# Comparisons for four users at a time in four slots, in place of eight users in two slots

## The chip, the cores and the metric

The kernel runs on one core of one Trainium2 chip. The metric is the device time of one execution in microseconds (us). A core has the matrix engine TensorE (PE in the rows; its weight loads are PEld), VectorE (DVE), ScalarE (ACT), GpSimd (POOL) and SyncE (SP). They run their own instruction streams and meet at semaphores. On-chip memory is SBUF (128 partitions) and PSUM, which TensorE writes. Tensors in DRAM are moved by DMAs, which here are issued by SP and by POOL.

## The reference

For 2048 users with a history of 200 item numbers each and 50 retrieved items each, over a table of 12500 items x 512:

```
mask = (sequence_ids != 0)
seq_emb = where(mask, item_embeddings[clip(sequence_ids - 1, 0)], 0)
pooled = seq_emb.sum(axis=1) / max(mask.sum(axis=1), 1)
user_rep = pooled @ W_rec.T + b_rec
retrieved = item_embeddings[retrieved_indices].mean(axis=1)
gate = sigmoid(concat([user_rep, retrieved]) @ gate_W.T + gate_b)
fused = gate * user_rep + (1 - gate) * retrieved
logits = fused @ proj_W.T + proj_b            # 2048 x 12500
```

## The kernel before

The histories are not gathered. Per user the kernel counts how often each of the 12544 table rows (98 chunks of 128) occurs, and multiplies the table by these counts. An item number is split into a chunk number and a row in the chunk. For each user, DVE compares the row keys of the 200 items with the numbers 0 to 127 and the chunk keys with 0 to 97 (`make_hots`, L568 and L570); TensorE multiplies the two zero-one matrices, which gives the 128 x 98 counts of that user (`count_quad`, L931, two matmuls a user), four users ("a quad") in one PSUM bank of three; ScalarE moves a quad to SBUF as bytes (`move_quad`, L779).

`make_hots(n)` makes one unit of 8 users: a DVE instruction of 2048 elements a partition into `row_hots` and one of 1568 into `chunk_hots`. There are two slots, so unit n waits until the quads of unit n-2 are counted (`quad_counted`). There are 4 groups of 512 users, each with 128 quads or 64 units.

The work runs in stages:

- Phase 0: group 0 is counted, with nothing to pool yet. The hots of all 64 units are made one after another. ScalarE squares a piece of the table after each seventh quad (L785), 14 times.
- Passes 0 to 3: pass g pools group g over 49 chunk pairs, 16 matmuls of 512 columns each pair (`pool_half`, L949), and in passes 0 to 2 TensorE counts the next group's quads between the half pairs (`quads_by`). On DVE, `units_by(i)` says how many units are made by iteration i of the pass. In pass 0 DVE also splits the table (`split_low`, L575). At the end of passes 0 and 1 DVE prepares the keys of the group after next (`prepare_ids`, L544 to L557), makes that group's first two units, and only then moves the pooled sums out of PSUM (`move_pooled`, L593), for which TensorE waits in the next pass.
- Logits: 400 blocks of 12 matmuls of 500 columns (L1022), moved by DVE (L755).

Beside this the 50 retrieved rows of each user are gathered by indirect DMAs from POOL, in program order. In a "lane" (`gather_lane`, L468 and L471) the DMA itself adds to what is there; there are 4 lanes of 50 gathers, two in phase 0 and pass 0, then one each during passes 1 and 2. The other blocks are gathered in batches of two (`gather_batch`, L449) into a pool of slots and added by DVE (`add_batch`, L610), 44 adds in pass 1 and 44 in pass 2, one after the hots of nearly each iteration. A batch that finds no free slot waits for an add. Turns of the first lanes wait for hots (L487), so that they are spread over phase 0 and pass 0. In pass 1 a turn of four lane gathers stands in front of each third batch until the lane is done.

Of the kernel before, what the change touches and what calls it, by code (L numbers as in the profile page):

```python
# [7 lines left out]
F16 = mybir.dt.float16  # L8
I32 = mybir.dt.int32
U8 = mybir.dt.uint8  # L10
ALU = mybir.AluOpType
# [3 lines left out]
P = 128  # L15
# [1 line left out]
KH = 4  # L17
H = 512
QUAD = 4
UNIT = 8  # L20
RING = 6
STAGE = 3
CVT = 3
# [28 lines left out]
class Plan:  # L52

    def __init__(self, seq_len, top_k, users, items, hidden):
# [7 lines left out]
        self.quads = G // QUAD  # L62
        self.units = G // UNIT
        self.width = next(n for n in range(512, 0, -1) if items % n == 0)
# [11 lines left out]
        return max(0, min(self.quads, (2 * i + half - 5) * self.quads // 90))  # L76

    def units_by(self, i):
        return min(self.units, self.quads_by(i + 1) // 2 + 1)

    def place_batches(self):

# [39 lines left out]
def pooling_program(nc, pl, ids, ret_ids, emb, w_rec_t, b_rec, w_gate_t, b_gate, proj_t, proj_b,  # L122
                    emb_parts, pool_dram, ret_dram, out):
    NQ, NP, NG, NB, K = pl.chunks, pl.pairs, pl.groups, pl.blocks, pl.top_k
# [4 lines left out]
    with ExitStack() as scope:  # L129
        def sem(name):  # L130
            return scope.enter_context(nc.semaphore(name))

        def sb(name, shape, dt):
            return scope.enter_context(nc.sbuf_tensor(name, shape, dt))
# [5 lines left out]
        keys = sb("keys", [P, 12288 + 2 * 8 * NQ * 2 * 2], U8)  # L140
        row_hots_t = sb("row_hots", [P, 2 * 8 * P * 2], F16)
# [20 lines left out]
        def part_of(tile, at, bytes_, dt):  # L162
            return tile[:, at:at + bytes_].bitcast(dt)
# [8 lines left out]
        clamped = part_of(keys, 4096, 4096, I32)  # L172
        row_key = part_of(keys, 8192, 2048, F16)
        chunk_key = part_of(keys, 10240, 2048, F16)
        chunk_hots = part_of(keys, 12288, 2 * 8 * NQ * 4, F16).rearrange("p (s k c v) -> p s k c v", s=2, k=8, v=2)
        row_hots = row_hots_t[:].rearrange("p (s k c v) -> p s k c v", s=2, k=8, v=2)
        present = sb("present", [P, 2 * G], F16)

        side = 2 * NQ * G // 2
# [52 lines left out]
        hots_made = sem("hots_made")  # L232
        quad_counted = sem("quad_counted")
# [67 lines left out]
        def adds_by_pass(g, i):  # L301

            if g <= 0:
                return 0
            return ADDS_PASS[g - 1] + min(ADDS_PASS[g] - ADDS_PASS[g - 1], (i + 1) * (ADDS_PASS[g] - ADDS_PASS[g - 1]) // 47)
# [123 lines left out]
        def _(pool):  # L429
# [31 lines left out]
            def gather_lane(block, turn):  # L461

                lane = block if block < LANES else 0
                for n in range(turn * LANE, min(turn * LANE + LANE, K)):
                    a = n % LANE
                    to, landed = gathered[:, lane * LANE + a], sum_in[lane][a]
                    if turn == 0:
                        pool.indirect_dma_start(to, None, source, column(block, n)).then_inc(landed, 16)  # L468
                    else:
                        pool.wait_ge(landed, lane_landed(block, a) - 16 * len(range(a, K, LANE)) + 16 * turn)  # L470
                        pool.indirect_dma_start(to, None, source, column(block, n), compute_op=ALU.add).then_inc(landed, 16)  # L471
# [12 lines left out]
            turns = -(-K // LANE)  # L484
            for turn in range(turns):
                if turn > 0:
                    pool.wait_ge(hots_made, 9 * turn)  # L487
                for block in range(LANES):
                    gather_lane(block, turn)
            pool.wait_ge(ret_rows_made, 2)  # L490
# [49 lines left out]
        def _(dve):  # L540
            def prepare_ids(g):
                dve.drain()
                dve.wait_ge(ids_in, 16 * (g + 1))
                dve.tensor_scalar(chunk_of, raw, -1.0, None, ALU.add)  # L544
                dve.tensor_scalar(chunk_key, raw, 0.0, ABSENT, ALU.is_equal, ALU.mult)
                if g > 0:
                    dve.wait_ge(present_counted, g)
                dve.tensor_scalar(present[:], raw, 0.0, None, ALU.not_equal)
                dve.drain()
                dve.tensor_scalar(clamped, chunk_of, 0.0, float(pl.items - 1), ALU.max, ALU.min)  # L550
                dve.drain()
                dve.tensor_scalar(raw, clamped, P - 1, None, ALU.bitwise_and)
                dve.tensor_scalar(clamped, clamped, 7, None, ALU.logical_shift_right)
                dve.drain()
                dve.tensor_tensor(row_key, raw, chunk_key, ALU.add)
                dve.drain()
                dve.tensor_copy(chunk_key, clamped)  # L557
                dve.drain().then_inc(ids_ready, 1)

            def make_hots(n):  # L560

                u = n % pl.units
                if n >= 2:
                    dve.wait_ge(quad_counted, 2 * (n - 1))
                rk = row_key[:, u * 16:u * 16 + 16].rearrange("p (k a v) -> p k a v", a=1, v=2)
                ck = chunk_key[:, u * 16:u * 16 + 16].rearrange("p (k a v) -> p k a v", a=1, v=2)
                cols = pair_columns[:].rearrange("p (a c) v -> p a c v", a=1)
                dve.tensor_tensor(row_hots[:, n % 2], cols.broadcast_to((P, 8, P, 2)),  # L568
                                  rk.broadcast_to((P, 8, P, 2)), ALU.is_equal)
                dve.tensor_tensor(chunk_hots[:, n % 2], cols[:, :, 0:NQ].broadcast_to((P, 8, NQ, 2)),  # L570
                                  ck.broadcast_to((P, 8, NQ, 2)), ALU.is_equal).then_inc(hots_made, 1)

            def split_low(i):
                dve.wait_ge(high_made, i + 1)
# [97 lines left out]
            dve.drain()  # L672
            dve.tensor_scalar(last_row, last_row_i, float(pl.items - 1), None, ALU.add)
            prepare_ids(0)
            make_hots(0)
            make_hots(1)
            def make_ret_rows(first, last):

                at = slice(first * K, last * K)
# [12 lines left out]

            dve.wait_ge(ret_ids_in, 16)
            make_ret_rows(0, LANES)
            for n in range(2, pl.units):
                make_hots(n)
                if n == 57:
                    dve.wait_ge(norm_summed, 1)
                    dve.tensor_reduce(small[:, 0:1], pooled_ps[:, 0, 0:NORM], AX.X, ALU.add)
                    dve.drain()  # L700
                    scale_from_squares(dve, small[:, 0:1], expo[:], small[:, 1:2], small[:, 2:3])
                    dve.drain().then_inc(scale_made, 1)
# [2 lines left out]
            split_low(2)  # L705
            prepare_ids(1)
            make_ret_rows(LANES, NB)
            make_hots(pl.units)
            make_hots(pl.units + 1)

            for g in range(NG):
                if g > 0:
                    move_pooled(g - 1)
                    make_recip(g)
                made = 2
                for i in range(NP):
                    if g == 0 and i == 0:
                        make_recip(0)
                    if g == 1 and i < LANES:
                        finish_lane(i)  # L720
                    if g >= 2 and i == 1:
                        finish_lane(g)
                    if g + 1 < NG:
                        while made < pl.units_by(i):
                            make_hots((g + 1) * pl.units + made)
                            made += 1
                    if g == 0 and i + 3 < NP:
                        split_low(i + 3)
                    before = adds_by_pass(g, i - 1) if i > 0 else adds_by_pass(g - 1, NP - 1)
                    for k in range(before, adds_by_pass(g, i)):  # L730
                        add_batch(k)
                    if g == NG - 1:
                        dense_step(i, MIX_PASS, SUM_PASS, LOW_PASS)
                        if i == 38:
                            scale_strip(0)
                        if i == 42:
                            low_strip(0)
                if g + 2 < NG:
                    prepare_ids(g + 2)
                    make_hots((g + 2) * pl.units)  # L740
                    make_hots((g + 2) * pl.units + 1)
            move_pooled(NG - 1)
            dve.drain()
            scale_out(0)
# [2 lines left out]
            for n in range(LAST):  # L747
                t, j = divmod(n, HALF_BLOCKS)
                r, v = divmod(n, ROWS)
# [161 lines left out]
        def _(pe):  # L911
# [8 lines left out]
                last.then_inc(present_counted, 1)  # L920

            def count_quad(q):
                pe.wait_ge(hots_made, q // 2 + 1)
                if q >= COUNT_BANKS:
                    pe.wait_ge(quad_moved, q - COUNT_BANKS + 1)
                slot = q // 2 % 2
                for u in range(QUAD):
                    pair, v = divmod(q % 2 * QUAD + u, 2)
                    to = count_ps[:, q % COUNT_BANKS, u * NQ:(u + 1) * NQ]
                    for part in range(2):  # L930
                        last = pe.matmul(to, row_hots[:, slot, pair * 2 + part, :, v],  # L931
                                         chunk_hots[:, slot, pair * 2 + part, :, v],
                                         start=(part == 0), stop=(part == 1))
                last.then_inc(quad_counted, 1)
# [184 lines left out]
```

## Time and profile before

| | |
|---|---|
| median of 3 runs | 2339.99 us (2335.43 to 2343.23) |
| profiled execution | 2341.4 us, its span 2339.7 us |
| mean granted TensorE clock | 0.949 |
| PE busy | 92% of the span |
| DVE busy | 64% |
| POOL busy | 48% |
| phase 0 (to the first pooling matmul) | 0 to 156 us |
| pass 0 | 156 to 388 us |
| pass 1 | 391 to 656 us |
| pass 2 | 661 to about 917 us |
| pass 3, then logits | to 1177 us, then to the end |

The stage borders are where the pooling matmuls of one pass end and those of the next begin in the timeline. A busy share is an average over stages with different limits, so each stage has to be read by itself.

### The profile page before, as it was taken

How to read it: one execution, taken by the hardware profiler on the slowest of the kernel's cores; microseconds unless marked ns; L12 is line 12 of the kernel's file. 1: busy time of each engine (PE TensorE's matmuls, PEld its weight loads, DVE VectorE, ACT ScalarE, POOL GpSimd, SP SyncE). 2: the span in 40 equal slices, each digit the busy share in tenths (PEclk: the TensorE clock that was granted, in tenths of full speed). 3: DMA queues.
4: the chain of work that ended last, by engine and by line, in shares of the span. 5: the costliest groups of instructions: out<-in, count | busy, mean ns of one | idle time of the engine just before them, and what ended most of it. 6: DMA issues, size and time to landing. Idle time of an engine off the chain costs nothing. (4 is left out here: it accounts for less than half of the span.)

```text
span 2339.7 us, 31173 instructions
## 1 busy us (share of the span) xinstructions
PE 2157.0 (92%) x12548; PEld 1099.0 (47%) x12548; DVE 1491.0 (64%) x1701; ACT 717.6 (31%) x947; POOL 1123.8 (48%) x830
## 2 busy tenths in 40 slices
PE   5669999888899888999999898999999999999999
PEld 4545555444545444444444343444444444444444
DVE  8998999676788766334477775876444444443343
ACT  6856775343444333222311111221121100111110
POOL 5673541888858888757368887788000000000000
PEclk7569999999999899999999999999999999999999
DMA  9998995999978999969588898888524445544553
GB/s 303 333 198 273 311 316 202 267 245 236 256 238 263 233 252 280 373 226 344 169 270 297 292 305 255 287 283 295 188 92 159 161 160 172 171 166 157 169 171 115
DMA packets 205198, 554.76 MB, mean 237 GB/s; under 512 B 20992, under 2 KB 104192, under 8 KB 201728
## 3 DMA queue, kind: packets, MB, share of 16 engines
q1 hardware_dynamic: 127424, 334.62, 41.3%
q0 software_dynamic: 77632, 218.16, 34.1%
q8 instruction: 101, 1.65, 0.3%
q14 instruction: 41, 0.34, 0.0%
HBM read 416.21 MB, written 136.48 MB: 236 GB/s over the span
## 5 line engine op out<-in xcount | busy, mean ns | idle before, releaser
L949 PE MATMUL pooled_ps<-mid,ring 128*128 128x512 f16 x3136 | 749.3, 388 | 20.9 <-DVE mid L593 7.9
L449 POOL DMA_INDIRECT gathered<-emb,ret_rows x462 | 565.9, 1225 | 236.8 <-issue 135.3
L755 DVE SCALAR_TENSOR_TENSOR ring<-pooled_ps,out_scale,counts 128x500 f32<-128x500 f32 x320 | 235.3, 736 | 355.4 <-PE pooled_ps L1022 351.0
L949 PEld LDWEIGHTS pooled_ps<-mid,ring 128*128 128x128 f16 x3136 | 298.3, 100 | 346.0 <-issue 54.4
L1022 PE MATMUL pooled_ps<-counts,keys 128*128 128x500 f16 x1920 | 427.5, 380 | 13.9 <-DVE ring L755 11.7
L471 POOL DMA_INDIRECT gathered<-emb,ret_rows x184 | 346.9, 1885 | 145.7 <-DVE keys L570 81.5
L1022 PE MATMUL pooled_ps<-counts,mid 128*128 128x500 f16 x1920 | 411.8, 374 | 0.0
L931 PE MATMUL count_ps<-keys,row_hots 128*128 128x98 f16 x4096 | 289.0, 228 | 108.1 <-DVE keys L570 92.6
L568 DVE TENSOR_TENSOR row_hots<-pair_columns,keys 128x2048 f16<-128x2048 f16 x256 | 312.6, 1221 | 60.3 <-PE count_ps L931 59.4
L931 PEld LDWEIGHTS count_ps<-keys,row_hots 128*128 128x128 f16 x4096 | 257.4, 109 | 191.9 <-DVE keys L570 108.7
L610 DVE TENSOR_TENSOR gathered<-gathered 128x1024 f32<-128x1024 f32 x182 | 223.2, 1226 | 158.0 <-DMA gathered<-emb,ret_rows 145.5
L779 ACT ACTIVATE counts<-count_ps 128x392 uint8<-128x392 f32 x512 | 237.6, 491 | 261.3 <-PE count_ps L931 261.2
L1022 PEld LDWEIGHTS pooled_ps<-counts,keys 128*128 128x128 f16 x1920 | 188.8, 100 | 240.9 <-issue 21.6
L861 ACT ACTIVATE counts<-counts,strip_scale 128x2000 f16<-128x2000 f32 x50 | 98.1, 1961 | 639.2 <-PE pooled_ps L1022 358.8
L1022 PEld LDWEIGHTS pooled_ps<-counts,mid 128*128 128x128 f16 x1920 | 186.8, 97 | 218.6
L803 ACT ACTIVATE mid<-counts 128x1024 f16<-128x1024 uint8 x196 | 205.9, 1054 | 184.9 <-PE pooled_ps L949 184.1
L570 DVE TENSOR_TENSOR keys<-pair_columns,keys 128x1568 f16<-128x1568 f16 x256 | 247.8, 968 | 0.0
L1022 PE MATMUL count_ps<-counts,keys 128*128 128x500 f16 x480 | 112.4, 385 | 9.9 <-DVE ring L755 8.5
L449 POOL DMA_INDIRECT counts<-emb,ret_rows x80 | 106.6, 1332 | 30.8 <-issue 23.5
L650 DVE SCALAR_TENSOR_TENSOR counts<-counts,strip_scale 128x2000 f16<-128x2000 f32 x50 | 114.7, 2293 | 0.0
L977 PE MATMUL count_ps<-counts 128*128 128x512 f32 x256 | 112.6, 593 | 0.0
L755 DVE SCALAR_TENSOR_TENSOR ring<-count_ps,out_scale,counts 128x500 f32<-128x500 f32 x80 | 58.9, 736 | 79.9 <-PE count_ps L1022 79.1
(96 smaller groups left out, 1036.6 us busy)
## 6 DMA issues: line engine op xcount, KB each, us to landing
logits<-ring SPq DMA_DIRECT2D x100, 1000.0 KB, 5.3
ring<-emb_parts SPq DMA_DIRECT2D x147, 512.0 KB, 5.6
counts<-proj_t SPq DMA_DIRECT2D x50, 1000.0 KB, 8.5
counts<-emb SPq DMA_DIRECT2D x14, 1792.0 KB, 10.5
mid<-emb SPq DMA_DIRECT2D x49, 512.0 KB, 8.1
emb_parts<-ring SPq DMA_DIRECT2D x49, 512.0 KB, 5.9
counts<-proj_b SPq DMA_DIRECT2D x50, 250.0 KB, 5.7
gathered<-emb,ret_rows POOLq DMA_INDIRECT x662, 5.8
```

The source lines that it names most:

```text
L449: pool.indirect_dma_start(slots[group][:, a], None, source, column(block, r * SLOT + a))\
L471: pool.indirect_dma_start(to, None, source, column(block, n), compute_op=ALU.add).then_inc(landed, 16)
L568: dve.tensor_tensor(row_hots[:, n % 2], cols.broadcast_to((P, 8, P, 2)), rk.broadcast_to((P, 8, P, 2)), ALU.is_equal)
L570: dve.tensor_tensor(chunk_hots[:, n % 2], cols[:, :, 0:NQ].broadcast_to((P, 8, NQ, 2)), ck.broadcast_to((P, 8, NQ, 2)), ALU.is_equal).then ...
L610: dve.tensor_tensor(slots[total], slots[total], slots[more], ALU.add).then_inc(added, 1)
L650: dve.scalar_tensor_tensor(strip_parts[:, t % 2, 1], strip[:, t % 2], strip_scale[:, c:c + 1], strip_parts[:, t % 2, 0], ALU.mult, ALU.sub ...
L755: dve.scalar_tensor_tensor(rows[:, r % ROW_SLOTS, v], logit_ps[n % BANKS][:, 0:W], out_scale[:, t % 2, j // 4:j // 4 + 1], bias[:, t % 2], ...
L779: act.activation(counts_v[:, g % 2, :, k * QUAD:(k + 1) * QUAD], count_ps[:, q % COUNT_BANKS, 0:QUAD * NQ].rearrange("p (u c) -> p c u", u ...
L803: act.activation(cvt[:, p % CVT], counts_v[:, g % 2, 2 * i:2 * i + 2], ACT.Copy).then_inc(cvt_made, 1)
L931: last = pe.matmul(to, row_hots[:, slot, pair * 2 + part, :, v], chunk_hots[:, slot, pair * 2 + part, :, v], start=(part == 0), stop=(part ...
L949: last = pe.matmul(pooled_ps[:, m], ring_v[:, p % RING, c, part, m * P:(m + 1) * P], cvt[:, p % CVT, c], start=(i == 0 and c == 0 and part ...
L1022: last = pe.matmul(logit_ps[n % BANKS][:, 0:W], fused[half][:, f, k, j * P:(j + 1) * P], strip_parts[:, t % 2, w, k, :], start=(k == 0 and ...
```

## The change

A unit becomes 4 users, that is one quad, and there are four slots of that size in the same memory. Each DVE instruction has half the elements (1024 and 784 a partition) and there are twice as many. The semaphore `hots_made` counts quads. Quad n waits for quad n-4; TensorE waits for just the quad it counts. The amounts at the other places (the start of a group, `units_by`, the turns of the lanes) are restated in quads.

```
-UNIT = 8
+UNIT = 4
+HOT_SLOTS = 4
...
     def units_by(self, i):
-        return min(self.units, self.quads_by(i + 1) // 2 + 1)
+        return min(self.units, self.quads_by(i + 1) + 2)
...
                 if turn > 0:
-                    pool.wait_ge(hots_made, 9 * turn)
+                    pool.wait_ge(hots_made, 18 * turn)
...
                 u = n % pl.units
-                if n >= 2:
-                    dve.wait_ge(quad_counted, 2 * (n - 1))
-                rk = row_key[:, u * 16:u * 16 + 16].rearrange("p (k a v) -> p k a v", a=1, v=2)
-                ck = chunk_key[:, u * 16:u * 16 + 16].rearrange("p (k a v) -> p k a v", a=1, v=2)
+                if n >= HOT_SLOTS:
+                    dve.wait_ge(quad_counted, n - HOT_SLOTS + 1)
+                rk = row_key[:, u * 8:u * 8 + 8].rearrange("p (k a v) -> p k a v", a=1, v=2)
+                ck = chunk_key[:, u * 8:u * 8 + 8].rearrange("p (k a v) -> p k a v", a=1, v=2)
                 cols = pair_columns[:].rearrange("p (a c) v -> p a c v", a=1)
-                dve.tensor_tensor(row_hots[:, n % 2], cols.broadcast_to((P, 8, P, 2)),
-                                  rk.broadcast_to((P, 8, P, 2)), ALU.is_equal)
-                dve.tensor_tensor(chunk_hots[:, n % 2], cols[:, :, 0:NQ].broadcast_to((P, 8, NQ, 2)),
-                                  ck.broadcast_to((P, 8, NQ, 2)), ALU.is_equal).then_inc(hots_made, 1)
+                dve.tensor_tensor(row_hots[:, n % HOT_SLOTS], cols.broadcast_to((P, 4, P, 2)),
+                                  rk.broadcast_to((P, 4, P, 2)), ALU.is_equal)
+                dve.tensor_tensor(chunk_hots[:, n % HOT_SLOTS], cols[:, :, 0:NQ].broadcast_to((P, 4, NQ, 2)),
+                                  ck.broadcast_to((P, 4, NQ, 2)), ALU.is_equal).then_inc(hots_made, 1)
...
-            make_hots(0)
-            make_hots(1)
+            for n in range(HOT_SLOTS):
+                make_hots(n)
...
             def count_quad(q):
-                pe.wait_ge(hots_made, q // 2 + 1)
+                pe.wait_ge(hots_made, q + 1)
                 if q >= COUNT_BANKS:
                     pe.wait_ge(quad_moved, q - COUNT_BANKS + 1)
-                slot = q // 2 % 2
+                slot = q % HOT_SLOTS
                 for u in range(QUAD):
-                    pair, v = divmod(q % 2 * QUAD + u, 2)
+                    pair, v = divmod(u, 2)
```

## Rows read from the trace of the kernel before

**Rows 1.** The page: busy time, share of span, instructions; clock by slice; a group.

```profile
PE 2157.0 (92%) x12548; PEld 1099.0 (47%) x12548; DVE 1491.0 (64%) x1701; ACT 717.6 (31%) x947; POOL 1123.8 (48%) x830
PEclk7569999999999899999999999999999999999999
L610 DVE TENSOR_TENSOR gathered<-gathered 128x1024 f32<-128x1024 f32 x182 | 223.2, 1226 | 158.0 <-DMA gathered<-emb,ret_rows 145.5
```

**Rows 2.** Busy by stretch: length, PE, PEld, DVE, ACT, POOL, clock, DMA share, GB/s.

```profile
11.07:152.00 140.93, 92.51 (x1022) 79.70 (x1023) 133.82 (x144) 103.35 (x155) 102.00 (x56) 0.58 1.00 282
177.00:387.60 210.60, 210.56 (x1754) 120.73 (x1754) 189.37 (x179) 146.32 (x215) 83.69 (x44) 0.99 0.92 292
401.80:636.00 234.20, 200.16 (x1613) 113.45 (x1611) 168.55 (x157) 94.90 (x160) 189.45 (x132) 0.94 0.91 249
695.00:897.00 202.00, 180.74 (x1453) 102.50 (x1451) 149.13 (x140) 85.91 (x144) 166.79 (x116) 0.95 0.92 255
```

**Rows 3.** Waits of DVE, 11 to 152 us: us in total, times, longest.

```profile
DVE row_hots L568 <- PE count_ps L931: 5.4, 14, 0.6
```

**Rows 4.** Timeline of DVE and POOL in phase 0: start, duration, instruction.

```profile
146.20 0.97 DVE L570 TENSOR_TENSOR keys<-pair_columns,keys 128x1568 f16<-128x1568 f16 x1
...
146.87 1.72 POOL L471 DMA_INDIRECT gathered<-emb,ret_rows  x1 [0.30 <-issue]
147.09 1.22 DVE L568 TENSOR_TENSOR row_hots<-pair_columns,keys 128x2048 f16<-128x2048 f16 x1
...
148.22 0.96 DVE L570 TENSOR_TENSOR keys<-pair_columns,keys 128x1568 f16<-128x1568 f16 x1
...
148.89 1.72 POOL L471 DMA_INDIRECT gathered<-emb,ret_rows  x1 [0.30 <-issue]
149.11 1.22 DVE L568 TENSOR_TENSOR row_hots<-pair_columns,keys 128x2048 f16<-128x2048 f16 x1
```

**Rows 5.** Waits of DVE in pass 0, 177 to 387 us.

```profile
DVE row_hots L568 <- PE count_ps L931: 18.5, 26, 2.1
```

**Rows 6.** Timeline at the border of passes 0 and 1.

```profile
377.48 1.23 DVE L568 TENSOR_TENSOR row_hots<-pair_columns,keys 128x2048 f16<-128x2048 f16 x1 [0.17 <-PE count_ps L931]
...
386.04 1.23 DVE L568 TENSOR_TENSOR row_hots<-pair_columns,keys 128x2048 f16<-128x2048 f16 x1
...
390.09 2.48 DVE L593 TENSOR_TENSOR mid<-pooled_ps,recip 128x512 f32<-128x512 f32 x4
390.92 3.29 PE L949 MATMUL pooled_ps<-mid,ring 128*128 128x512 f16 x8 [3.33 <-DVE mid L593]
```

**Rows 7.** Waits of POOL and PE, 401.8 to 636 us.

```profile
POOL gathered L449 <- issue: 18.9, 62, 0.3
...
POOL gathered L449 <- DMA ret_dram<-gathered: 5.7, 2, 4.6
PE count_ps L931 <- DVE keys L570: 34.0, 10, 8.7
```

**Rows 8.** Line 449 alone by stretch: length, POOL busy, clock, DMA share, GB/s.

```profile
401.80:636.00 234.20, 97.31 (x80) 0.94 0.91 249
695.00:897.00 202.00, 83.60 (x70) 0.95 0.92 255
```

**Rows 9.** Line 471 alone by stretch; its form: min/median/max ns.

```profile
401.80:636.00 234.20, 85.38 (x46) 0.94 0.91 249
695.00:897.00 202.00, 76.96 (x41) 0.95 0.92 255
L471 POOL DMA_INDIRECT gathered<-emb,ret_rows x46: 1534/1704/2524, 428.9 to 627.6; - x46
```

**Rows 10.** Timeline in pass 1: two gathers, the DVE instruction, a later count.

```profile
420.19 0.97 DVE L570 TENSOR_TENSOR keys<-pair_columns,keys 128x1568 f16<-128x1568 f16 x1
420.26 1.72 POOL L449 DMA_INDIRECT gathered<-emb,ret_rows  x1 [0.30 <-issue]
423.86 0.94 POOL L449 DMA_INDIRECT gathered<-emb,ret_rows  x1 [0.30 <-issue]
433.88 0.83 PE L931 MATMUL count_ps<-keys,row_hots 128*128 128x98 f16 x8 [5.72 <-DVE keys L570]
```

More of the change, by code:

```diff
@@ L174, in pooling_program @@
         chunk_key = part_of(keys, 10240, 2048, F16)
-        chunk_hots = part_of(keys, 12288, 2 * 8 * NQ * 4, F16).rearrange("p (s k c v) -> p s k c v", s=2, k=8, v=2)
-        row_hots = row_hots_t[:].rearrange("p (s k c v) -> p s k c v", s=2, k=8, v=2)
+        chunk_hots = part_of(keys, 12288, 2 * 8 * NQ * 4, F16).rearrange("p (s k c v) -> p s k c v", s=HOT_SLOTS, k=4, v=2)
+        row_hots = row_hots_t[:].rearrange("p (s k c v) -> p s k c v", s=HOT_SLOTS, k=4, v=2)
         present = sb("present", [P, 2 * G], F16)
@@ L694, in _ @@
             make_ret_rows(0, LANES)
-            for n in range(2, pl.units):
+            for n in range(HOT_SLOTS, pl.units):
                 make_hots(n)
-                if n == 57:
+                if n == 114:
                     dve.wait_ge(norm_summed, 1)
@@ L707, in _ @@
             make_ret_rows(LANES, NB)
-            make_hots(pl.units)
-            make_hots(pl.units + 1)
+            for n in range(pl.units, pl.units + HOT_SLOTS):
+                make_hots(n)
             for g in range(NG):
@@ L714, in _ @@
                     make_recip(g)
-                made = 2
+                made = HOT_SLOTS
                 for i in range(NP):
@@ L739, in _ @@
                     prepare_ids(g + 2)
-                    make_hots((g + 2) * pl.units)
-                    make_hots((g + 2) * pl.units + 1)
+                    for n in range((g + 2) * pl.units, (g + 2) * pl.units + HOT_SLOTS):
+                        make_hots(n)
             move_pooled(NG - 1)
```

## The prediction

> **What bounds the kernel now.** I read the page first [rows 1]: PE is busy for 92% of the span, so the change, which only touches how DVE feeds the counting, can matter only where PE is held up. The clock by slice says where: it is low in the first three slices (phase 0) and near full after, with small dips. Then the table of stretches [rows 2], one line a stage. From 11 to 152 us PE is busy 92.5 of 141 us at a clock of 0.58 (mostly the lower of its two levels), DVE 133.8: phase 0 is bound by DVE. From 177 to 388 us PE is busy all the time and DVE for 189 of 211: pass 0 is bound by PE, with DVE close behind. From 402 to 636 us (pass 1) and 695 to 897 us (pass 2) no engine is full by the table, but POOL has 189.5 us of work in 132 gathers, and the list of waits [rows 7] shows that POOL's other time is the fixed 0.30 us between two gathers and 5.7 us for a store: 132 x 0.30 = 40 us, 189.5 + 40 = 229 of 234 us. So POOL never stops there. PE stops 10 times for 34 us for hots, because DVE stands in an add whose gather has not landed and the hots are queued behind it. I read passes 1 and 2 as bound by POOL's stream of gathers, and the stalls of PE as its form.
>
> **Phase 0, the price of twice the instructions.** The recorded durations, 1.22 and 0.97 us, overlap: from start to start a row compare takes 148.22 - 147.09 = 1.13 us and a chunk compare 149.11 - 148.22 = 0.89, together 2.02 us for 8 users [rows 4]. The difference of 480 elements is 0.25 us, 0.52 ns each. 2048 elements are then 1.07 us, and about 0.07 us is fixed per instruction (1568: 0.82 and 0.07). Halved, the two are 0.60 and 0.48 us, 1.08 a quad or 2.16 for 8 users: +0.14 us a unit. 64 units: +9.1 us of DVE, all of it on the path. The wait for a counted quad stays hidden when it is met: the row compare at 149.11 has one in front and starts at the usual distance [rows 4]. What goes away: DVE waits 5.4 us, 14 times, for counts [rows 3], once for each of the 14 squares on ScalarE. Now it needs both quads of the last but one unit before it may start either new one. With single quads it can make one more quad meanwhile, worth over 1 us against stalls of 0.6 at most, so I take all 5.4 away (bounds 0 and 5.4). Phase 0: +9.1 - 5.4 = +3.7 us (bounds +2 and +9.1). A bound for the fixed part from the other side is the recorded duration less the elements, 1.22 - 1.07 = 0.15 us for each instruction.
>
> The first quad is ready a unit's half earlier, but PE waits for the next ones at once; nothing. Between phase 0 and pass 0 DVE works in one chain and makes four quads for two units: +0.3 us, against which the last quads are counted sooner, about 0.5 us. -0.2 us.
>
> **Pass 0.** DVE gets 64 x 0.14 = 9 us more. It now waits 18.5 us for PE [rows 5] in 26 places and is idle 21 us [rows 2]; PE does not wait for it. The cover is that slack: +0 us. If the slack were gone (fixed part 0.15, so +0.30 a unit and 19 us) it would be just used up.
>
> **Borders of passes 0/1 and 1/2.** PE waits 3.3 us for `move_pooled` [rows 6], which starts at 390.09 at the end of an unbroken DVE chain whose beginning is the last unit's hots at 377.48, and that start waited for PE. The wait of the last quad (124 quads counted) is the same as that of the last unit now, but behind it stands one quad of 1.08 us and not a unit of 2.02: -0.94. The four early quads are 4.32 for 4.04 us: +0.28. -0.66 each, -1.3 us.
>
> **Passes 1 and 2, the gathers.** A gather that starts with DVE idle takes 0.94 us; one that starts at 420.26, 0.07 after a compare that ends at 421.16, takes 1.72 and ends 0.82 us after that end [rows 10]. In phase 0 the gather of 146.87 ends 1.42 us after the compare's end at 147.17 [rows 4]. So a gather is held once, at its start, until the running DVE instruction ends. Shorter compares hold it less. The Trainium skill (SBUF — State Buffer, section "Who interferes with whom") has this as an exclusive lock on a port pair that VectorE and GpSimd share, held for a whole instruction, and says that a VectorE instruction with two SBUF inputs contends only with a GpSimd instruction that reads SBUF; by its remark that `tensor_tensor` did not stall DMA descriptors nothing would be gained here. That part the row of 420.26 speaks against.
>
> How much: line 449 has 80 gathers in 97.3 us in pass 1 [rows 8]; at 0.945 each they would be 75.6, so 21.7 us are holding. In pass 2, 83.6 - 66.2 = 17.4. Line 471 has a least time of 1.54 [rows 9]: 85.4 - 70.8 = 14.6 and 77.0 - 63.1 = 13.8. Not all of this is due to compares. A start at random into an instruction of length L is held for L²/2 per instruction in sum: a unit (1.13² + 0.89²)/2 = 1.03, an add 1.22²/2 = 0.74 [rows 1]. 64 units and 44 adds make 66 and 33, so two thirds are due to the compares. Two quads have 0.60² + 0.48² = 0.59 for 1.03: 43% less. For line 449 this is (21.7 + 17.4) x 0.67 x 0.43 = 11.3 us less, for line 471 8.2 less if its starts were random. They aren't: in rows 4 a held gather ends 1.42 us after an end, the next comes 0.30 later and is held to the unit's end, so one gather takes 2.02 us, one unit. With ends at 0.60, 1.08, 1.68 and 2.15 us it would be held to 2.15 us. So for line 471 the lock step gives +0.13 x 87 = +11 us at most, random starts -8; I take 0, between them. As POOL sets the pace, the 11.3 us come off the path: PE has 34 us of stalls in pass 1 to give [rows 7].
>
> When an add lets go, PE gets its first quad after 1.08 us of compares and not 2.02. In the middle of a pass POOL's pace decides and this is worth nothing; at the last stall of pass 2 it should be worth about 0.9: -1 us.
>
> Pass 3 and the logits have no compares: 0.
>
> **The sum.** +3.7 - 0.2 + 0 - 1.3 - 11.3 - 1 = -10.1 us, from the profiled execution's 2341.4: 2331.3. That execution stands 1.4 us above the median of 2340.0; I don't correct for it and say 2331.
>
> **The rivals.**
> - *The gathers are not faster* (in the lanes and outside the start just falls into another compare). Then only the rest is left: +3.7 - 0.2 - 1.3 - 1 = +1.2, 2342.6. For it: the gathers are not random but follow DVE's ends. Against it: no compare can then hold a gather for more than 0.6 us, where one now is held 0.8 [rows 10].
> - *Starts are random in the lanes too*: another -8.2, 2323. For it: between adds and waits for PE, DVE's pattern in passes 1 and 2 is ragged.
> - *Lock step on the lanes, slower.* In turns of four lane gathers DVE has just been let go and works without a break, so the pattern of rows 4 is repeated, at 2.15 for 2.02 us; 87 gathers give +11, and without a gain on line 449: 2341.4 + 1.2 + 11 = 2354. It decides if DVE runs compares for more than two gathers on end (over 4 us), which it does after a long stall but not with an add and a wait in each iteration.
> - *The fixed part is whole.* If instructions half as long no longer overlap, the price is 0.30 us a unit: 64 x 0.30 = 19 for 9 us in phase 0, pass 0's slack just covers it. With the gain on the gathers 2331 + 10 = 2341, without it 2353. The two neighbours in rows 4 that overlap by 0.08 us speak against it. The Trainium skill (VectorE: DVE Perf Modes, section "The TRN2 errata — SBUF-src ops pay a fixed extra latency per instruction") has about 151 cycles at 0.96 GHz fixed for each such instruction, the recorded durations agree with that, and by it as a start-to-start price phase 0 would be 20 us dearer.
>
> That PE loses by counting single quads I rule out: it issues the same matmuls in the same order.
>
> **How the numbers follow.** The forecast 0.48; gathers no faster 0.20; random in the lanes too 0.15; lock step, slower 0.10; fixed part whole 0.07. A measurement tells about 0.3% from no change, 7 us: faster is below 2333, slower above 2347. The forecast's own spread is 6 us (phase 0 from 0 to +9, line 449 from 6 to 15 us), so of its 0.48 0.35 is faster and 0.13 the same; with the random case 0.15 that is 0.50 faster. Same: 0.13 + 0.18 + 0.03 = 0.34. Slower: 0.10, 0.04 and 0.02 of the others, 0.16. The range goes up to 2354, and down to the random case with phase 0 at 0 and line 449 at 15 us, 2323 - 3.7 - 3.7 = 2316, less 4 for the dips of the clock behind the stalls [rows 1], for which I take a tenth of the 34 us of stalls [rows 7]: 2312.
>
> **What would show it.** In phase 0 compares of 0.60 and 0.48 us from start to start and first pooling matmul near 160 us, DVE's 5.4 us of waits gone. Pass 0 still with no stall of PE. `move_pooled` at the borders 0.7 us nearer to the last count. Line 449 at a mean near 1.14 for 1.22 us in pass 1, line 471 near 1.86 as now, POOL still without waits, pass 1 shorter by about 6 us and pass 2 by 5. The prediction is wrong if POOL is as busy as now or passes 1 and 2 do not follow POOL; if DVE's slack in pass 0 is in the wrong places and PE waits; or if phase 0 grows by over 9 us.

## The result

| | before | after |
|---|---|---|
| median | 2338.32 us (4 runs, 2335.43 to 2343.23) | 2354.47 us (4 runs, 2351.83 to 2357.38) |
| ratio | | 1.0066 (95% interval 1.0045 to 1.0087) |
| span of the profiled execution | 2339.7 us | 2350.5 us |

The changed kernel is slower by 0.7%, where 2331 us and faster was forecast. After its first 48 matmuls of pass 0 PE stops for the split table and then takes the pass up again (before, then after); this second start is called the resumption below:

```profile
176.99 3.57 PE L949 MATMUL pooled_ps<-mid,ring 128*128 128x512 f16 x8 [7.75 <-DVE ring L575]
178.92 3.55 PE L950 MATMUL pooled_ps<-mid,ring 128*128 128x512 f16 x8 [8.64 <-DVE ring L576]
```

By stages, from pooling matmul to pooling matmul in the two timelines, the 10.8 us between the two spans are made up so: the resumption at 178.92 for 176.99 (+1.9), pass 0 from there 241.1 for 213.9 (+27.2), pass 1 262.6 for 270.0 (-7.4), pass 2 252.0 for 257.8 (-5.8), pass 3 257.5 for 258.7 (-1.2), logits 1158.4 for 1162.2 (-3.8). So there is one large loss, in the one stage that I had costed at nothing, and three steps near their forecast.

The page of after, busy time, clock by slice and a group, beside [rows 1]:

```profile
PE 2163.0 (92%) x12548; PEld 1093.4 (47%) x12548; DVE 1524.0 (65%) x2213; ACT 712.2 (30%) x947; POOL 1193.4 (51%) x830
PEclk9569999999999999999999899999999999999999
L472 POOL DMA_INDIRECT gathered<-emb,ret_rows x184 | 434.8, 2363 | 94.9 <-DMA gathered<-emb,ret_rows 52.6
```

POOL's busy time has grown by 70 us for the same 830 instructions, and the mean of the lane gathers is 2.36 us (it was 346.9 us in 184, 1.89 each). The busy table by stretch (length, PE, PEld, DVE, ACT, POOL, clock, DMA share, GB/s), beside [rows 2]:

```profile
11.07:155.00 143.93, 102.66 (x1028) 79.36 (x1028) 142.67 (x273) 105.32 (x158) 130.20 (x17) 0.69 0.60 205
178.92:420.00 241.08, 216.21 (x1754) 119.42 (x1755) 202.47 (x311) 142.84 (x216) 135.02 (x80) 0.99 1.02 299
420.00:682.60 262.60, 229.26 (x1810) 128.36 (x1811) 209.82 (x321) 106.85 (x177) 198.38 (x147) 0.95 0.88 252
682.60:934.60 252.00, 228.40 (x1810) 127.95 (x1811) 200.57 (x305) 105.58 (x176) 191.62 (x139) 0.96 0.88 247
```

In phase 0 POOL is busy for 130 us with 17 instructions, where it was busy for 102 with 56, and the DMAs moved 205 GB/s instead of 282. In pass 0 POOL has 80 instructions for 44, the DMA engines are full (share 1.02) and PE, full before, has 25 us of gaps. POOL's timeline names the instruction, and DVE's the moment at which it ends:

```profile
28.86 1.25 POOL L469 DMA_INDIRECT gathered<-emb,ret_rows  x1 [0.30 <-issue]
32.80 105.89 POOL L472 DMA_INDIRECT gathered<-emb,ret_rows  x1 [2.69 <-DVE keys L571]
...
136.67 0.55 DVE L571 TENSOR_TENSOR keys<-pair_columns,keys 128x784 f16<-128x784 f16 x1
...
137.14 0.15 DVE L700 TENSOR_REDUCE small<-pooled_ps 128x1 f32<-128x14 f32 x1
...
137.38 0.15 DVE L1062 TENSOR_SCALAR expo<-small 128x1 int32<-128x1 int32 x1
...
139.00 1.57 POOL L472 DMA_INDIRECT gathered<-emb,ret_rows  x1 [0.30 <-issue]
```

One lane gather takes 105.9 us: it is shut out. It stands from 32.80 to 138.69, while DVE makes compares without a break, and ends 1.47 us after the end of the last compare at 137.22, at which DVE turns to a chain of tiny instructions. A held lane gather ended 1.42 us after a compare's end in [rows 4], so it was let in there. The reduction at 137.14 starts 0.08 us before that compare ends, so by its time the end of the row of compares let it in, not a gap. Everything behind it on POOL is late: 18 gathers have begun before the first pooling matmul, and 90 between that and pass 1; before it was 58 and 50. The waits of 180 to 420 us show what 40 more gathers do there (us in total, times, longest):

```profile
ACT ring L794 <- DMA mid<-emb: 81.1, 38, 4.5
POOL gathered L472 <- DMA gathered<-emb,ret_rows: 52.6, 53, 5.8
...
DVE ring L576 <- ACT ring L794: 36.6, 38, 3.2
...
PE count_ps L932 <- ACT counts L780: 21.0, 31, 3.0
...
DVE row_hots L569 <- PE count_ps L932: 1.5, 2, 0.9
```

The table's loads (`mid<-emb`) come late, ScalarE waits 81 us for them, DVE behind it, and PE behind ScalarE's move of the counts. DVE's waits for counts have fallen from 18.5 [rows 5] to 1.5 us: it is no longer held by PE but by DMAs.

### The profile page after: what moved, and what is told of

Read it like the earlier page. It is cut to its first block and busy times, and to the rows that moved or that the text cites. A ratio compares the mean times of both kernels' runs of the same rounds, so it can differ in the third digit from the quotient of the medians.

```text
span 2350.5 us, 31685 instructions
## 1 busy us (share of the span) xinstructions
PE 2163.0 (92%) x12548; PEld 1093.4 (47%) x12548; DVE 1524.0 (65%) x2213; ACT 712.2 (30%) x947; POOL 1193.4 (51%) x830
## 5 line engine op out<-in xcount | busy, mean ns | idle before, releaser
L450 POOL DMA_INDIRECT gathered<-emb,ret_rows x462 | 549.2, 1189 | 235.2 <-issue 134.6
L472 POOL DMA_INDIRECT gathered<-emb,ret_rows x184 | 434.8, 2363 | 94.9 <-DMA gathered<-emb,ret_rows 52.6
L932 PE MATMUL count_ps<-keys,row_hots 128*128 128x98 f16 x4096 | 296.4, 227 | 113.0 <-DVE keys L571 77.3
L569 DVE TENSOR_TENSOR row_hots<-pair_columns,keys 128x1024 f16<-128x1024 f16 x512 | 349.6, 683 | 12.2 <-PE count_ps L932 11.4
L780 ACT ACTIVATE counts<-count_ps 128x392 uint8<-128x392 f32 x512 | 232.5, 490 | 218.4 <-PE count_ps L932 218.4
L571 DVE TENSOR_TENSOR keys<-pair_columns,keys 128x784 f16<-128x784 f16 x512 | 285.5, 558 | 0.0
```

What stands on the lines that cost most here:

```text
L450: pool.indirect_dma_start(slots[group][:, a], None, source, column(block, r * SLOT + a))\
L569: dve.tensor_tensor(row_hots[:, n % HOT_SLOTS], cols.broadcast_to((P, 4, P, 2)), rk.broadcast_to((P, 4, P, 2)), ALU.is_equal)
L571: dve.tensor_tensor(chunk_hots[:, n % HOT_SLOTS], cols[:, :, 0:NQ].broadcast_to((P, 4, NQ, 2)), ck.broadcast_to((P, 4, NQ, 2)), ALU.is_equ ...
L780: act.activation(counts_v[:, g % 2, :, k * QUAD:(k + 1) * QUAD], count_ps[:, q % COUNT_BANKS, 0:QUAD * NQ].rearrange("p (u c) -> p c u", u ...
```

## The experiments

They are in three groups: what makes pass 0 longer, what shuts the gather out, and what shorter compares are worth in passes 1 and 2. Diffs are against the changed kernel unless said otherwise. Stage lengths are between the same matmuls as above.

### Pairs of quads in phase 0

The edit, shortened:

```
+                w = 2 if n < 128 else 1      # two quads in one instruction pair, odd n returns
...
-                dve.tensor_tensor(row_hots[:, n % HOT_SLOTS], ...
+                dve.tensor_tensor(row_hots[:, 4 * s:4 * (s + w)], cols.broadcast_to((P, 4 * w, P, 2)), ...
```

> The changed kernel, but in phase 0 two quads are again made by one instruction pair of 2048 and 1568 elements into two neighbouring slots; passes 0 to 2 keep single quads. Theory A (one lane gather is shut out for 106 us by unbroken short compares of phase 0, the lane gathers then fall into pass 0 and fill the DMA engines there): no gather over 3 us, some 56 gathers in phase 0 as before, pass 0 back from 241 to about 214 us, about 2325 us in all. Rival B (pass 0 is longer because of its own short compares): the long gather may go, but pass 0 stays near 241 us, about 2350 in all.

2324.9 us beside 2343.1, ratio 0.992 (0.9901 to 0.9939). Pass 0 from the resumption is 212.9 us, with 57 gathers in phase 0 and 51 behind it. The lane gathers of phase 0 in one row (min/median/max ns):

```profile
L477 POOL DMA_INDIRECT gathered<-emb,ret_rows x49: 1541/1717/2552, 32.3 to 154.5; - x49
```

Pass 0 still makes single quads and has lost its 27 us. Rival B falls: the short compares of pass 0 cost it nothing, as forecast. This form brings back both the long compares and DVE's waits, so it doesn't say which of them keeps the gathers from being shut out.

### A drain before each eighth quad of phase 0

```
+                if n < 128 and n % 8 == 0:
+                    dve.drain()
```

> The changed kernel with a drain of VectorE in front of each eighth quad in phase 0, and nothing else. Theory A: the drain leaves a short gap each 8.7 us in which the gather gets through, so the longest gather is at most about 9 us and pass 0 is between 214 and 225 us; total 2327 to 2338. If the gap of a drain is too short for a gather, one gather stays near 106 us and the total near 2354. Rival B: about 2354 whatever the gathers do.

2329.4 us, ratio 0.9946 (0.9931 to 0.9961); pass 0 212.5 us. The timeline of a gather that is shut out and let in (rows between are left out; DVE's go on in the same rhythm):

```profile
53.15 5.46 POOL L472 DMA_INDIRECT gathered<-emb,ret_rows  x1 [2.57 <-DVE keys L573]
...
56.63 0.56 DVE L573 TENSOR_TENSOR keys<-pair_columns,keys 128x784 f16<-128x784 f16 x1
...
57.28 0.69 DVE L571 TENSOR_TENSOR row_hots<-pair_columns,keys 128x1024 f16<-128x1024 f16 x1
```

Neighbouring compares overlap by 0.08 us in the records. Here 0.09 us lie between 57.19 and 57.28, and the gather ends at 58.61, 1.42 us after 57.19. The longest gather of phase 0 is 5.58 us. A gap of a tenth of a microsecond is enough.

### The kernel before, with its lane gathers late

```
 (against the kernel before)
-                    pool.wait_ge(hots_made, 9 * turn)
+                    pool.wait_ge(hots_made, max(9 * turn, 57))
```

> The kernel before, with units of 8 users in two slots, but the lane gathers after the first turn wait until 57 units are made, near 135 us. That puts the same gathers into pass 0 as in the changed kernel, with the old compares. Theory A: pass 0 grows from 214 to about 240 us with the DMA engines full, total 2338 + 26 = 2364. Rival B: pass 0 stays at 214 us and the total at 2338.

2367.5 us, ratio 1.0096 (1.0069 to 1.0123). 18 gathers in phase 0 and 90 behind it, as in the changed kernel, and the same pass 0:

```profile
176.70:417.30 240.60, 217.63 (x1754) 121.36 (x1754) 192.69 (x184) 143.62 (x216) 145.83 (x81) 0.97 1.02 300
```

240.6 us, DMA share 1.02, 300 GB/s, with the old compares. So late gathers by themselves cost pass 0 its 27 us; with the two runs before, nothing is left for the rest of the change.

### The kernel before, each compare in two halves

```
 (against the kernel before)
+                for h in range(2):
+                    at = slice(4 * h, 4 * h + 4)
+                    dve.tensor_tensor(row_hots[:, n % 2, at], ...)
+                    last = dve.tensor_tensor(chunk_hots[:, n % 2, at], ...)
+                last.then_inc(hots_made, 1)
```

> The kernel before, each compare cut in two halves of four users, still units of 8 users, two slots and the old waits. It separates the size of the instructions from the slots and waits. Theory A with gaps (the waits for counts, 5.4 us in phase 0, let gathers in): short compares but no gather over about 10 us; phase 0 longer by 9 us, passes 1 and 2 shorter by 7 us each as in the changed kernel, total about 2335. If the short compares alone shut the gather out whatever the waits: a gather of 40 us or more and a pass 0 of about 240, total about 2360.

2332.5 us, ratio 0.9953 (0.9936 to 0.9971). The lane gathers of phase 0, and DVE's waits there:

```profile
L471 POOL DMA_INDIRECT gathered<-emb,ret_rows x49: 1541/1852/4367, 33.0 to 153.5; - x49
DVE row_hots L570 <- PE count_ps L934: 1.1, 7, 0.2
```

Short compares alone do not make a gather of 40 us or more. With two slots DVE still waits for counts, 7 times for 0.2 us, and no gather is shut out for more than 4.4 us. Three of the four over 3.2 us end 1.42 us after the end of a compare that has such a gap behind it; the fourth, which starts at 32.99 and takes 3.36 us, is let in at the end of a compare with no gap behind it. In the changed kernel DVE has no such wait in phase 0.

The timelines of all runs together (30 to 152 us) tell what the size does and what the gaps do. The five kernels with long compares in phase 0 have 41 lane gathers that start into a compare after a pause of POOL of over 0.7 us; each is let in at the end of that compare, though for 31 of them DVE's next gap is over 2 us away. The nine kernels with short compares have 24 such gathers, and 15 of them are held beyond that compare, 4 of 8 in this run. So it is the short compares that let a gather be shut out, and the gaps set for how long. Pass 0 is 214.1 us, passes 1 and 2 are 266.3 and 251.7. The resumption is at 181.0, 4 us later than before.

### The same with another release of POOL

Four runs ask what decides that a gather is shut out. The first lets POOL go by the counts:

```
-                    pool.wait_ge(hots_made, 18 * turn)
+                    pool.wait_ge(quad_counted, 18 * turn)
```

> The changed kernel, but the lane turns wait for the counts of the same quads and not for their compares, so that POOL is let go some 0.8 us later in VectorE's cycle; VectorE's work is untouched. In the changed kernel the gather that is shut out starts 0.34 us after the start of a row compare, as each one that a compare lets go. Theory (the shut-out depends on the phase at which the gather starts): no gather over 10 us, pass 0 near 213 us, total 2325 to 2330. Rival (unbroken short compares shut out any lane gather that waited): a gather of about 100 us again and about 2354.

2357.9 us, ratio 1.0061 (1.004 to 1.0082), pass 0 241.0 us:

```profile
34.30 104.28 POOL L472 DMA_INDIRECT gathered<-emb,ret_rows  x1 [4.31 <-PE count_ps L932]
```

The second waits for one quad more (`18 * turn + 1`):

> The changed kernel, the lane turns wait for one quad more (18 n + 1). The release comes one quad later but at the same place in VectorE's cycle. Theory of the phase: shut out again, a gather of about 105 us, pass 0 near 241, about 2354. Rival (a chance meeting at one moment): no long gather, about 2327.

2353.9 us (one execution), one gather of 104.8 us, pass 0 240.7 us. The third puts a tiny instruction in front:

```
                     pool.wait_ge(hots_made, 18 * turn)
+                    pool.memset(nap[:, turn:turn + 1], 0.0)
```

> The changed kernel with a memset of one element on POOL in front of each lane turn in phase 0 and pass 0, behind its wait. The release stays; only the gather's start moves on by the memset, 0.1 us or more. Theory of the phase: no gather over 10 us, about 2327, unless the memset moves it by a whole quad of 1.08 us. Rival: a gather of about 100 us and about 2354.

2350.5 us (one execution):

```profile
32.69 0.10 POOL L490 MEMSET nap<- 128x1 f32 x1 [2.48 <-DVE keys L573]
...
32.94 105.86 POOL L473 DMA_INDIRECT gathered<-emb,ret_rows  x1
```

The fourth takes the waits away:

```
-                if turn > 0:
-                    pool.wait_ge(hots_made, 18 * turn)
```

> The changed kernel without the waits that spread the lane turns of the first two lanes over phase 0 and pass 0; VectorE's work is untouched. In the runs so far each gather that was shut out for over 3 us in phase 0 stood behind a wait of POOL of 1.4 us or more, and none that followed the one before it by 0.3 us. Theory C (a gather that follows at once is not shut out): no gather over 4 us in phase 0, about 65 gathers there at 2.15 us each, pass 0 at 213 to 220 us, total 2325 to 2335. Rival (any gather can be shut out by unbroken short compares): a gather of many tens of us and about 2354.

2349.1 us, ratio 1.0046 (1.0027 to 1.0064), pass 0 233.4 us with 74 gathers:

```profile
62.89 1.85 POOL L472 DMA_INDIRECT gathered<-emb,ret_rows  x1 [0.30 <-issue]
65.56 73.05 POOL L472 DMA_INDIRECT gathered<-emb,ret_rows  x1 [0.82 <-DMA gathered<-emb,ret_rows]
```

My theory of the phase falls: a gather is shut out from four places in DVE's cycle (0.34 and 0.39 us into a row compare, 0.15 and 0.29 us into a chunk compare), and in the run with halved compares four that started 0.35 or 0.36 us into a row compare behind a pause were not (1.73 to 1.75 us each). The wait for one quad more agreed with it and doesn't save it. Theory C held for gathers that follow at once, but its forecast for the lanes without waits was wrong, since POOL also pauses there for a gather that has not landed. What is left is an observation: every gather that stood for tens of microseconds came after a pause of POOL, of 0.82 us here and 1.5 to 4.3 in the others (with the memset, the pause lies in front of the memset), and none that followed the one before by 0.30 us did. Why that is so, and why some after a pause get through, stays open.

### One drain

```
+                if n == 22:
+                    dve.drain()
```

> The changed kernel with one drain of VectorE in phase 0, in front of quad 22, some 4 us after the gather that is shut out has begun. Theory (a gather once shut out leaves only at a gap of VectorE): the first lane gather behind a wait ends about 1.4 us after the drain's gap, so it takes 5 to 6 us; a later gather behind a wait can be shut out again, until the next gap at 137 us. If no later one is, total about 2327 and pass 0 at 213; if the next turn's first gather at about 52 us is, it takes about 85 us, some 64 gathers are left for pass 0 and the total is near 2345.

2344.1 us (one execution), POOL's timeline:

```profile
32.62 5.52 POOL L472 DMA_INDIRECT gathered<-emb,ret_rows  x1 [2.69 <-DVE keys L573]
38.44 1.57 POOL L472 DMA_INDIRECT gathered<-emb,ret_rows  x1 [0.30 <-issue]
...
68.34 1.85 POOL L472 DMA_INDIRECT gathered<-emb,ret_rows  x1 [0.30 <-issue]
71.68 66.98 POOL L472 DMA_INDIRECT gathered<-emb,ret_rows  x1 [1.49 <-DVE keys L573]
```

The first gather is let in by the drain after 5.5 us, 15 more pass at 2.15 us each, and the next one behind a pause is shut out until the row of compares ends at 137 us, 67 us long. Both parts of the theory hold here: the drain's gap frees the gather, and the trap is there again for the next. 74 gathers are left for pass 0, which takes 229.1 us; with 90 it is 241 and with 50 it is 213.9, about 0.65 us for each gather. The run without waits has 74 gathers too and takes 233.4.

### What the shorter compares are worth in passes 1 and 2

The edit, shortened as above:

```
 (against the run gated on counts)
+                w = 2 if n >= 256 else 1
```

> As the run that gates the lanes on counts, but the hots that are made in passes 1 and 2 are again pairs of quads (2048 and 1568 elements). It prices the shorter compares where POOL sets the pace. Theory (short compares hold gathers less): passes 1 and 2 back from 262.6 and 252.0 to about 270 and 258 us, total 12 us above that run. Rival (the gain there comes from elsewhere): both passes as short as there, within 3 us.

2373.3 us, ratio 1.0143 (1.0123 to 1.0162), 15 us above the run gated on counts. Passes 1 and 2 take 271.1 and 260.4 us, where that run has 265.2 and 251.6; phase 0 and pass 0 are alike, with a gather of 104.3 us in each. The gathers of the batches alone in these passes (length, POOL busy), first the run gated on counts, then this one:

```profile
419.90:685.20 265.30, 108.33 (x94) 0.95 0.88 249
685.20:936.80 251.60, 101.86 (x86) 0.96 0.88 249
```

```profile
420.20:691.20 271.00, 110.91 (x94) 0.93 0.87 244
691.20:951.60 260.40, 107.97 (x86) 0.95 0.86 238
```

The gain of single quads is in these two passes, and the gathers are faster: 8.7 of the 14.7 us by these rows, the rest lies in lane gathers and in PE getting its first quad sooner, which I did not separate.

The other profiles, one of each form, show how sure this is. Pass 1 takes 262.6 to 270.8 us (mean 266.0) in the eleven forms with short compares there and 270.0 to 271.3 in the three with long ones; pass 2 takes 249.9 to 253.9 against 257.8 to 260.4. The gain in pass 2 is clear. That of pass 1 is about 5 us on average, and two forms with short compares there (pairs in phase 0 alone with 270.3, pairs to the end of pass 0 with 270.8) don't show it.

### Towards a faster version

> Pairs of quads in phase 0, single quads in the passes (the fastest form so far, 2325 us beside 2343), and no waits between the lane turns. If the spreading of the lanes has no use of its own, about 2325; if the gathers then crowd the DMA engines in phase 0, where the table's norm is loaded too, phase 0 grows by up to 5 us, 2325 to 2330. It looks for a version that beats both kernels.

2337.6 us beside 2339.1, ratio 0.9996 (0.9984 to 1.0008). No gather is shut out, but pass 0 takes 225.1 us, 12 more than with the waits, with as many gathers (57 and 51). The DMA traffic from 200 to 400 us, in 40 slices, suggests why:

```profile
GB/s 302 300 303 302 302 301 301 301 302 299 304 299 304 340 420 412 329 234 217 216 258 303 252 237 210 213 211 319 198 223 234 233 246 232 213 210 126 141 325 370
```

Ungated, the lanes' rest runs back to back at the start of pass 0 and the DMA engines stand at 302 GB/s for a third of it. The waits between turns have a use.

> The changed kernel, but the compares of phase 0 and of pass 0 are made for two quads at once (2048 and 1568 elements), and single quads only in passes 1 and 2, where POOL's gathers set the pace. Theory: phase 0 and pass 0 as in the kernel before (resumption at 177 us, pass 0 213 us), passes 1 and 2 shorter by 7 and 6 us, so 2338 to 2341 less 13: ratio 0.993 to 0.996. If the single quads of pass 0 had a part in the gain of the form with pairs in phase 0 alone (0.992), this one is nearer to 1.

Ratio 0.9962 (0.9922 to 1.0001), 2352.5 us beside 2365.1 on a chip that was slower for both. Pass 0 is 216.6 us in its profile, 213 was expected, and passes 1 and 2 are 270.8 and 249.9 us, where pass 3 took 287.9, 25 us more than in any other profile, which I can't explain. This doesn't separate it from pairs in phase 0 alone, nor clearly from no change.

Pairs in phase 0 and single quads in the passes, 0.992 by four executions, is the fastest form found, and faster than both kernels.

## Why the prediction was wrong

- **What bounds each stage:** right for phase 0, pass 1 and pass 2. For pass 0 right for the kernel before; I saw the DMA share of 0.92 in [rows 2] and did not ask how much room it left.
- **Phase 0:** right. The compares take 0.60 and 0.48 us from start to start (12.18, 12.78 and 13.26 in the timeline), DVE's 5.4 us of waits are gone, and PE resumes 1.9 us later for 3.5 forecast. The rival of a whole fixed part is out.
- **Pass 0 at +0: the step that failed.** It cost +27.2. I priced DVE's slack as the only cover. The real cover was that POOL had issued 58 gathers in phase 0, and the change took that away. I had written for phase 0 that the 5.4 us of waits go, and booked it as a gain; with them went the last gaps on DVE, which would have ended a shut-out soon. I asked of each gather how long one instruction holds it, never whether it may be held by the next as well. That was also the premise of "a gather is held once, at its start", which the rows I had chosen could only show for long compares; for short ones 15 of 24 gathers behind a pause were held beyond the first compare.
- **Borders:** wrong, small. PE waits 3.80 and 5.53 us for the moved sums, where it was 3.33 [rows 6] and 4.53, and not 0.66 less. At the first border DVE's chain no longer started from a wait for PE (the group's last compare ended at 408.54, the move began at 419.18).
- **Passes 1 and 2:** right in this profile, -7.4 and -5.8 for about -6 and -5; over all profiles about -5 and -7. Line 449's mean in pass 1 went from 117.12/94 = 1.246 to 1.139 us for 1.14 forecast, and the lane gathers from 1.856 to 1.836 for 1.86, by these rows of after (line 450, then 472):

```profile
420.00:682.60 262.60, 107.11 (x94) 0.95 0.88 252
420.00:682.60 262.60, 84.45 (x46) 0.95 0.88 252
```

  In pass 2 line 449's mean went from 106.37/87 = 1.223 to 100.76/86 = 1.172, less than in pass 1.

- **Pass 3 and logits:** 0 forecast, -5.0 in the profiled executions. Nothing in them was changed, and the logits alone range from 1155.9 to 1164.0 us over the profiles of this study; I take it for the spread.
- **The rivals:** the slower one named 2354, and 2354 was measured, by chance. Its lock step is there (in phase 0 a lane gather takes 2.15 us where one took 2.02) but phase 0 has room for it, and in passes 1 and 2 the lane gathers did not get slower. No rival had the shut-out. Without it the sum was about right: with the trap taken out of phase 0 two ways, 18.2 us (pairs in phase 0) and 13.7 us (drains) below the kernel before on the same chip were measured, where the sum had 10.1, or 13.8 without the dearer compares of phase 0 that the pairs avoid.

## What to carry to other kernels

A stage that is "hidden" behind another may depend on a third engine's work done ahead of time; when a change makes an engine's instructions shorter and its stream denser, list who gets in between them and in the gaps before booking the removal of waits as a gain. A change of instruction size is best made where it pays (here where POOL's gathers set the pace) and left out where it does not. In a profile, compare busy time with the count of instructions: 130 us for 17 was visible at once.

## What the runs showed of the hardware

- A gather issued by POOL (indirect DMA) is held at its start by a VectorE compare with two SBUF inputs until that instruction ends: 0.94 us free, 1.72 held. The Trainium skill (SBUF — State Buffer, section "Who interferes with whom") has that `tensor_tensor` did not stall DMA, with a reason that is marked as inferred; for these gathers, which read their row numbers from SBUF, that did not hold.
- An adding gather can be shut out for as long as an unbroken row of such instructions of 0.60 and 0.48 us goes on: 105.9, 104.3, 104.8, 104.3, 105.9, 73.1 and 67.0 us were seen, each ending 1.42 to 1.48 us after the end of the row's last compare. Gaps of 0.09 to 0.16 us let it in too, and one shut out for 3.36 us got in without any. With compares of 1.13 and 0.89 us no lane gather of phase 0 took over 2.6 us, though the gaps were 6 to 12 us apart.
- The fixed cost from one of these VectorE compares to the next was 0.07 us, though each is recorded with 0.15 us beyond its elements (1024 elements: 0.60 us from start to start, 0.68 recorded, at 0.52 ns an element).
- With the table's loads and stores and lane gathers at once the DMA engines stood at 299 to 304 GB/s for 65 us on end (the run with pairs and no waits), and in the changed kernel ScalarE waited 81.1 us of pass 0 for the table's loads.
